# A four-layer graph network on one core: x fetched at the end of the preceding group, a third PSUM bank for the similarity blocks, and another order of loads and mixing at the start of the next pass

## What is computed

```python
def _L1_gnn_ref(x, adj, weight, bias):
    h = x @ weight
    norm = jnp.linalg.norm(h, axis=1, keepdims=True)
    h_norm = h / jnp.maximum(norm, NORM_EPS)
    sim = h_norm @ h_norm.T
    attn_logits = sim / TAU + jnp.log(adj + EPS)
    attn = jax.nn.softmax(attn_logits, axis=1)
    return attn @ h + bias

h = relu(layernorm(x)); x = x + L0(h, adj, W)        # relu(A_norm @ (A2 @ h @ W.T))
h = relu(layernorm(x)); x = x + L1(h, adj, weight, bias)
h = relu(layernorm(x)); x = x + L2(h, adj, W, b)     # relu(normalised adj @ h @ W + b)
h = relu(layernorm(x)); x = x + L3(h, adj, W1, W2)   # two graph convolutions
```

## Time and profile before

| | before |
|---|---|
| time, median of 3 runs | 2350.82 us (2348.93 to 2351.11) |
| time of the profiled execution | 2350.55 us |
| its span, first to last instruction | 2348.8 us |
| granted TensorE clock, mean | 0.998 |
| TensorE busy | 2308.0 us (98%) |
| VectorE busy | 1718.9 us (73%) |
| ScalarE busy | 1131.4 us (48%) |
| moved by DMA | 726.86 MB, mean 309 GB/s |

### The profile page before, as it was taken

How to read it: one execution, slowest core, us unless ns; L and a number is a source line. 1 busy time by engine, 2 the same in 40 slices (tenths; PEclk the granted TensorE clock), 3 DMA queues, 4 the chain that set the end, 5 groups by cost and what they waited for, 6 DMA issues and landing times. The chain is left out here.

```text
span 2348.8 us, 62852 instructions
## 1 busy us (share of the span) xinstructions
PE 2308.0 (98%) x24536; PEld 1936.3 (82%) x24536; DVE 1718.9 (73%) x2765; ACT 1131.4 (48%) x1821; POOL 140.4 (6%) x114
## 2 busy tenths in 40 slices
PE   7999999999999999999999999999999999999999
PEld 6888887666666677777778799999988888899998
DVE  7877867677777777678878967676776766667665
ACT  6634443445544555555545545545554444433332
POOL 2211101101100000000000000000000000000000
PEclk9999999999999999999999999999999999999999
DMA  8699998889887988989999999899898898999997
GB/s 287 223 361 335 355 361 298 254 263 283 274 262 226 263 282 281 280 259 308 320 294 314 298 354 328 302 340 334 302 335 328 316 350 309 329 348 382 373 378 290
DMA packets 291738, 726.86 MB, mean 309 GB/s; under 512 B 76704, under 2 KB 109728, under 8 KB 258848
## 3 DMA queue, kind: packets, MB, share of 16 engines
q1 hardware_dynamic: 291328, 724.42, 89.2%
q10 hardware_dynamic: 288, 0.79, 0.1%
HBM read 574.64 MB, written 138.41 MB: 304 GB/s over the span
## 5 line engine op out<-in xcount | busy, mean ns | idle before, releaser
L931 PE MATMUL acc<-right,ahi 128*128 128x258 f16 x1536 | 419.8, 273 | 4.9 <-DVE o L1742 2.1
L933 PE MATMUL acc<-right,alo 128*128 128x258 f16 x1536 | 419.3, 273 | 0.0
L932 PE MATMUL acc<-right,ahi 128*128 128x256 f16 x1536 | 418.7, 273 | 0.0
L953 PE MATMUL acc<-left,ahi 128*128 128x128 f16 x1536 | 272.0, 220 | 3.7 <-DVE alo L1726 3.7
L957 PE MATMUL acc<-left,alo 128*128 128x128 f16 x1536 | 272.1, 220 | 0.0
L956 PE MATMUL acc<-left,ahi 128*128 128x128 f16 x1536 | 272.0, 220 | 0.0
L1580 ACT ACTIVATE ahi<-en 128x512 f16<-128x512 f32 x256 | 160.3, 626 | 91.2 <-DVE en L2066 88.3
L931 PEld LDWEIGHTS acc<-right,ahi 128*128 128x128 f16 x1536 | 150.2, 98 | 41.2 <-DVE alo L2081 9.8
L928 PE MATMUL acc<-left,ahi 128*128 128x512 f16 x512 | 180.2, 379 | 0.0
L928 PE MATMUL acc<-left,en 128*128 128x512 f16 x512 | 180.2, 379 | 0.0
L953 PE MATMUL acc<-left,adj 128*128 128x128 f16 x1024 | 179.0, 220 | 0.0
(11 more groups left out here) (255 smaller groups left out, 6546.1 us busy)
## 6 DMA issues: line engine op xcount, KB each, us to landing
adj<-in_adj_t SPq DMA_DIRECT2D x192, 512.0 KB, 6.1
adj<-ready SPq DMA_DIRECT2D x96, 1024.0 KB, 7.7
en<-ready SPq DMA_DIRECT2D x96, 1024.0 KB, 7.7
adj<-in_adj_t SPq DMA_DIRECT2D x32, 1024.0 KB, 8.3
en<-in_adj_t SPq DMA_DIRECT2D x32, 1024.0 KB, 8.8
en<-ready SPq DMA_DIRECT2D x64, 512.0 KB, 5.4
en<-sent SPq DMA_DIRECT2D x46, 512.0 KB, 6.9
sent<-en SPq DMA_DIRECT2D x90, 256.0 KB, 4.3
```

The lines of the kernel that those rows point to most:

```text
L931: nc.tensor.matmul(acc[:, b, 0:n], hi, m[:, jb, 0:n], start=first, stop=False)
L932: nc.tensor.matmul(acc[:, b, 0:F], hi, m[:, jb, LO:LO + F], start=False, stop=False)
L933: return nc.tensor.matmul(acc[:, b, 0:n], lo, m[:, jb, 0:n], start=False, stop=last)
L953: nc.tensor.matmul(to, hi[:, rows], bhi[:, cols], start=first and i % 2 == 0 and b == 0 and k == 0, stop=False, skip_group_check=True)
```

## The change

Four things change.

1. `fetch_x(ATT, g)` moves from half 3 of group g + 1 to half 15 of group g. For the last group it moves from chunk 2 of pass 3 to half 15 of group 7.
2. From the second group on, similarity blocks use three banks in turn, `psS[0]`, `psS[1]` and `psX`, except blocks 23 to 29, around the weight product that needs `psX`; there they use two. TensorE gets waits so that `psX` is free (`sim_taken`, `small_copied`).
3. SyncE's loads at the start of pass 3 are in another order: the prepared parts of chunk 0 come ahead of the fresh parts of chunks 1 to 3, and fresh and prepared parts then alternate.
4. In the last group only, `mix0`, `mix1`, `mix2` and `W2` of group 6 leave VectorE's blocks 26 to 30 (and ScalarE's block 28) and stand in chunks 0 to 2 of pass 3.

```diff
+        sim_banks = [psS[:, 0, :], psS[:, 1, :], psX]
...
+        W_AT = 23
+        SIM_SLOT, SIM_BEFORE = [], []
+        for n in range(NG * NB):
+            last = {s: m for m, s in enumerate(SIM_SLOT)}
+            s = min((0, 1) if n < NB or W_AT <= n % NB < W_AT + 7 else (0, 1, 2), key=lambda s: last.get(s, s - 3))
+            SIM_SLOT.append(s)
+            SIM_BEFORE.append(last.get(s))
...
+        def sim_taken(eng, n):
+
+            g, j = divmod(n, NB)
+            if not turned(g, j):
+                eng.wait_ge(exp_ready, exp_no(g, j))
+            else:
+                eng.wait_ge(num_ready, n + 1)
...
             def str_group(p, g, now, before):
                 first = p == STR[0] and isinstance(g, int) and g == 0
                 for c in range(NC):
-                    if not (first and c < 4):
+                    if not (first and c < 2):
                         load_fresh(p, g, c)
                     if not (first and c == 0):
                         load_ready(p, g, c)
-                    if c == 1 and first:
+                    if c == 2 and first:
                         store_s4(NG * NC - 1)
-                    if c == 2 and now[0] in BACK:
+                    if c == 2 and now[0] in BACK and not first:
                         fetch_x(*now)
...
-                    if H == 3:
-                        fetch_x(ATT, g - 1)
-                    elif H == 8:
+                    if H == 8:
                         send_x(ATT, g - 1)
                     elif H == 12:
                         turn_h(ATT, g - 1)
+
+                if H == NH - 1:
+                    fetch_x(ATT, g)
...
                     load_fresh(STR[0], 0, 0)
                     store_s4(NG * NC - 3)
-                    for c in range(1, 4):
-                        load_fresh(STR[0], 0, c)
                     load_ready(STR[0], 0, 0)
+                    load_fresh(STR[0], 0, 1)
                     store_s4(NG * NC - 2)
...
-                before = (g, j - 2) if j >= 2 else (g - 1, j - 2 + NB)
-                if before[0] >= 0:
-                    if not turned(*before):
-                        pe.wait_ge(exp_ready, exp_no(*before))
+                before = SIM_BEFORE[n]
+                if before is not None:
+                    sim_taken(pe, before)
+                if SIM_SLOT[n] == 2:
+                    if n < NB + W_AT:
+                        pe.wait_ge(gn_ready, at([1], 1, NG - 1, GB, GB))
                     else:
-                        pe.wait_ge(num_ready, n - 1)
+                        pe.wait_ge(small_copied, at(COPIED, ATT, (n - W_AT) // NB - 1, GB, GB))
...
-                           16: ["h0"], 18: ["h1"], 26: ["mix0"], 27: ["mix1"], 28: ["mix2"], 29: ["sum"], 30: ["W2"],
-                           31: ["split0"]}]
+                           16: ["h0"], 18: ["h1"], 29: ["sum"], 31: ["split0"]}]
+            LATE = {0: ["mix0", "mix1"], 1: ["mix2"], 2: ["W2"]}
```

More of the change, by code:

```diff
@@ L401, in exp_no, with sim_bank @@
             return sum(NB - GB * h for h in range(g)) + j - GB * g + 1
+        W_AT = 23
[5 more added lines that the diff above has]
+            SIM_BEFORE.append(last.get(s))
+        def sim_bank(g, j):
+            return sim_banks[SIM_SLOT[g * NB + j]]
+        def sim_taken(eng, n):
[4 more added lines that the diff above has]
+                eng.wait_ge(num_ready, n + 1)
         def sent_no(g, H):
@@ L1041, in small @@
                 elif p == 3 or p == ATT and isinstance(g, int) and g == NG - 1:
+                    if p == ATT:
+                        pe.wait_ge(num_ready, NG * NB)
                     pe.wait_ge(hT_kept, turned_at(p, g) + 2)
@@ L1046, in small @@
                     pe.wait_ge(hT_landed, 16 * at(TURN, p, g))
+                    if p == ATT:
+                        sim_taken(pe, max(n for n in range((g + 1) * NB + W_AT) if SIM_SLOT[n] == 2 or n == 0))
                 if not isinstance(g, int) or g > 0:
@@ L1099, in _ @@
                     START_PLACES[q - 2, i] = [(name, q)]
-            ATT_PLACES = [{14: "W0W1"}, {23: "W0W1"}]
+            ATT_PLACES = [{14: "W0W1"}, {W_AT: "W0W1"}]
             def moving_there(p, g, c):
@@ L1148, in similarity @@
                     for b in range(k):
-                        last = nc.tensor.transpose(psS[:, j % 2, b * P:(b + 1) * P],
+                        last = nc.tensor.transpose(sim_bank(g, j)[:, b * P:(b + 1) * P],
                                                    exp_of(g, GB * g + b)[:, k * P:(k + 1) * P], ident32[:, :])
@@ L1548, in group @@
                         hi_of_s3(g - 1, NC - 1)
+                    if tp == ATT and c == 1:
+                        hi_of_mixT(ATT, NG - 2)
                     for name in PLACES.get(c, []):
@@ L1558, in exponential @@
                 first = turned(g, j) * P
-                nc.scalar.activation(exp_of(g, j)[:, first:], psS[:, j % 2, first:], ACT.Exp,
+                nc.scalar.activation(exp_of(g, j)[:, first:], sim_bank(g, j)[:, first:], ACT.Exp,
                                      scale=1.0 / (GN_SCALE * GN_SCALE)).then_inc(exp_ready, 1)
@@ L2037, in group @@
                         split(p, g, c)
+                    if tp == ATT:
+                        for name in LATE.get(c, []):
+                            if name == "W2":
+                                stage(name, ATT, NG - 2)
+                            else:
+                                att_piece(name, NG - 2)
                     for name in PLACES.get(c, []):
@@ L2056, in numerators @@
                     dve.wait_ge(sim_ready, n + 1)
-                    pieces.append((psS[:, j % 2, :], 0, split_at))
+                    pieces.append((sim_bank(g, j), 0, split_at))
                 if split_at < GR:
```

5 lines of the change are left out of this document (2 added, 3 removed).

## The result

The changed kernel takes 2329.48 us (median of 4 runs, 2328.68 to 2330.57), the one before 2349.90 us in the same session (4 runs, 2348.93 to 2351.11). The ratio is 0.9913, its 95% interval 0.9896 to 0.9930. The profiled execution took 2330.06 us with a span of 2328.3 us, 20.5 us less than the span before.

The account below looks back on a forecast made before the run. TensorE, busy 98% of the span, was taken as the bound, so only its pauses and slow stretches could be won. 14.9 + 0.6 + 1.3 + 3.8 + 2.8 - 0.4 = 23.0 us off 2350.82 gave 2327.8 us, range 2325 to 2331.

Parts of the forecast that it names:

- load of x, groups 2 to 7: Attention group starts: an earlier load ends VectorE's waits for x and TensorE's behind them; gain 14.9 us.
- third bank: Attention group starts: gains only where the bank waits for a computed similarity block; 0 to 0.6 us, taken as 0.6.
- waits of blocks 30 and 31: End of pass 2: without the mixing, TensorE's waits of 2.0 us fall to 0.7; gain 1.3 us.
- step into pass 3: Start of pass 3: earlier prepared load gains 3.8 us, steady clock 2.8, added mixing costs 0.4.
- 3.8 us would stay: Group starts: of TensorE's 18.7 us of waits, 3.8 us remain because VectorE itself sets the pace at blocks 5 to 10.
- Waits at chunks 2 and 3: Pass 3: listed as a sign of being wrong, though chunk 3 was estimated 0.4 us late.
- the stand for x in pass 3 covers the mixing: Pass 3, chunks 0 to 2: VectorE's 8.36 us wait for x covers 3.5 us of added mixing; cost 0.4 us.
- The queue: Rival, attention pass: transfers set the pace and half of 15.5 us is lost, giving 2335.6 us; chance 0.12.
- that rival: End of pass 2: clock falls anyway or the next load is late, 2.8 us not won, 2330.6 us; chance 0.10.
- Three banks pull no clock down: Judges a rival: three banks lower the clock at group starts, 12.6 us over seven groups, 2340.4 us; chance 0.02.
- ScalarE's copies of the weight product: Rival, before similarity block 30: TensorE waits for these copies; 2357.9 us if they came 10 us late; chance 0.01.
- the prediction's ground for a steady clock: Start of pass 3: a 0.7 us pause should not lower the clock, since 2 us pauses did not; gain 2.8 us.

Follow-up runs that it names:

- e1: Kernel before with only the load of x moved to the end of the group before: 2338.43 us, ratio 0.9941.
- e4: Changed kernel with the third bank taken out again, two banks throughout: 2331.13 us, ratio 0.9913 against the kernel before.
- e3: Kernel before with the new order of loads at the start of pass 3 and the mixing moved into pass 3: 2346.61 us, ratio 0.9985.
- e2: Kernel before with only the third bank added: 2352.78 us, ratio 1.0009.
- e7: Kernel before with the load of x at half 2 in place of half 3, the one of pass 3 left: 2338.81 us, ratio 0.9946.
- e5: Kernel before with only the order of loads at the start of pass 3 changed: 2346.20 us, ratio 0.9985.
- e6: Kernel before with only the mixing moved into pass 3, order of loads kept: 2351.72 us, ratio 1.0001.
- e9: Kernel before with new load order, moved mixing and pass 3's load of x early; attention groups' loads of x stay at half 3: 2343.43 us, ratio 0.9973.
- e10: Changed kernel with the loads of x back at half 3 and chunk 2 of pass 3: 2350.62 us, ratio 0.9995 against the kernel before.
- e11: Changed kernel with VectorE's low part and difference of block 1 reordered at the start of pass 2: 2330.70 us, ratio 0.9914 against the kernel before.
- e8: Changed kernel with mixed output's low part behind chunk 3 and the statistics' mean at block 11: 2330.04 us, ratio 0.9909 against the kernel before.
- e12: Changed kernel with VectorE's additions one block earlier at the start of pass 2, block 1's difference behind block 2: 2328.84 us, ratio 0.9909 against the kernel before.

## Why the prediction was right, point by point

**The sum.** 23.0 us were forecast and 20.5 measured by the spans. With the stretches of e1 and e4 beside those of before and after, the gain can be told apart by terms:

| term | forecast, us | measured, us | from |
|---|---|---|---|
| load of x, groups 2 to 7 | 14.9 | 14.2 | before less e1: 11.67 + 2.54 |
| third bank | 0.6 | 0.4 | e4 less after: 0.43 in groups 2 to 6 |
| waits of blocks 30 and 31 | 1.3 | 1.0 | e1 less e4, group 7: 0.97 |
| step into pass 3 | 3.8 + 2.8 - 0.4 = 6.2 | 6.1 | before less after |
| start of pass 2 | none | -1.25 | after less before |

Every stretch is of one profile. With x late, groups 2 to 6 differ from profile to profile (368.25 us in e3, 370.08 in e2), so the first term is known to some 2 us only; with x early they agree within 0.1 us among the kernels with as many banks.

**The load of x and the third bank.** The chain (late x, late VectorE, late TensorE) is shown by e1 and e7. The forecast took VectorE's waits as the measure of what TensorE gets back, 2.56 us a group, and that came out within the 2 us. The waits in the trace themselves are a rough measure. In groups 2 to 6, those of the weight loads fell from 15.2 to 2.0 us, 13.2 us for a gain of 12.09: a little too much. Those in the matmuls' own rows fell from 9.3 to 1.2 us, 8.1 us: far too little, since the matmul's record hides a part of a short wait. At 1289.49 us the matmul's row has 0.41 where the load's has 0.65:

```profile
1289.49 0.28 PE L952 MATMUL acc<-right,ahi 128*128 128x258 f16 x1 [0.41 <-DVE alo L2115]
```

The 20 waits of 0.18 us in the earlier trace rows, 3.5 us, do not show in the matmuls' rows at all. They can't all have been free of cost: without them the weight loads' waits of groups 2 to 6 are 12.4 us, of which e1 leaves 2.1, and that is less than the 11.67 us that e1 gained. That 3.8 us would stay was right in kind: 2.6 stayed.

**The end of the pass.** The load as releaser, against the name in the row, is shown by e1, e5 and e6. The clock stayed at 1.00 at the start of pass 3; the three terms of the step are measured only as a sum. In e1 and e7, where x is early and the prepared load late, the pause is there (4.63 and 4.82 us) and the clock falls as before. The wait at chunk 3 is 0.56 us for the 0.4 of the forecast. "Waits at chunks 2 and 3" stood among the signs of being wrong, although a small one was forecast: as a sign it was drawn too wide.

**The start of pass 2.** The 1.25 us lost there are no effect of the change but of the clock, which stayed up in the profile of before and fell in that of the changed kernel behind the same pause. The forecast had no term for it, and it rested on a profile in which the clock had stayed up. That this did not carry the time out of the stated range is the margin of the range, not foresight.

**The terms are not independent.** The prediction said that the stand for x in pass 3 covers the mixing. It is more than that. With x late, order and mixing together gain no more than the order alone (e3 and e5, both 0.9985). The step into pass 3 shows where it goes: 32.01 us before, 27.96 with the order alone, 30.22 with order and mixing, where the wait moves to chunk 2 and the clock fell behind it in this profile, and 25.91 once x is early too (e9). The early x takes the standing out of VectorE and makes room for the mixing. One at a time the four edits give by their ratios 0.59 - 0.09 + 0.15 - 0.01 = 0.64%, 15 us; together 0.87%, 20.4 us. And all but the first give 0.05% (e10).

**The rivals.** The queue does not pace the pass: in groups 2 to 6 the DMA share went from 0.91 to 0.92 and TensorE is busy 356.68 of 357.93 us. The clock did fall, but at the start of pass 2 and not at its end, where that rival had it. Three banks pull no clock down: groups 2 to 7 stand at 1.00. On the rule of the Trainium skill ("TensorE: Matmul & The Clock Gate", section "A second HAM failure mode: psum-queue depth-cycling"), that micro-pauses while PSUM banks are cycled make the clock go to and fro, e2 and the changed kernel show nothing of it here. TensorE did not wait for ScalarE's copies of the weight product in any group.

## What to carry to other kernels

A wait at a buffer (here a PSUM bank) says who was late, not that the buffer is short: follow the late engine to its own wait, and a load issued a few us earlier (4 in e7) may be worth far more than the deeper buffer, which here mostly renamed the wait. Edits around one hand-over are not a sum. Moving work behind a hand-over pays only if the engine that gets it has no wait of its own there, and moving a late load pays only as far as the next late thing lets it. Size a gain by the distance of two landmarks: here the weight loads' waits overstated it by a tenth and the matmuls' own understated it by a third. And test a releaser that a row names when something else ends at nearly the same time.

## What the runs showed of the hardware that I had not expected

- The granted clock does not follow from the pause alone. At 748 us, behind the same pause of 2.3 us (e11: 2.45) and the same work, it fell in 9 of 13 profiled executions (after, e1, e2, e4 to e8, e11) and stayed in 4 (before, e3, e9, e10). Elsewhere it fell behind 2.35 us (e9, 1224.59 us), 3.26 (e3), 3.38 and 5.14 (e10) and 3.48 (e6), and stayed behind 2.37 (e3), 2.34 and 2.59 (e5) and 3.58 (e2). Behind none of the pauses of 2.0 us or less at the group starts did it fall. So the prediction's ground for a steady clock, that pauses of 2 us had not moved it, was sound only just. Behind the longest pauses at the end of pass 2 it fell each time: 3.99 us (before), 4.43 (e2), 4.63 (e1), 4.82 (e7) and 5.83 (e6). What decides between 2.3 and 3.6 us is not settled. The fall at 748 us costs 1.3 to 1.7 us: from the entry of pass 2 to group 1 it is 85.3 us in the four profiles in which the clock stayed, and 86.6 to 87.0 in the nine in which it fell. That a part of the spread of the times goes with the pauses is likely but not shown: before had 2345.55 to 2354.73 us in 21 runs, e12 0.23 us in four. The row of e9 behind its 2.35 us:

```profile
1224.00:1228.00 4.00, 3.40 (x17) 0.60 1.07 409
```

- The profile twice named an engine's instruction where something else released TensorE: a DMA (L1726 in the earlier trace rows), and VectorE's additions out of the accumulators in place of the low part, where the load's row and the matmul's row name different ones.
- In the step into pass 3 of the changed kernel the transfers ran at 396 GB/s over 25.90 us with a share of 1.01, and no wait of an engine there names a load.
